# Placing tokens behind a step's first layer, with chunk 1's gates after the gathers and nine leading units

## What is computed

```
xn = layernorm(x)
s = group_norm(tanh(relu(rope(xn @ W_Q)) + hh_b))          # then turned
idx, w = route(xn)              # sigmoid, 4 of 8 groups, 6 of 32 experts, w sums to 2.5
gate[t, idx[t]] = w[t]
moe = sum_e gate[:, e] * (square(relu(xn @ W1[e].T)) @ W2[e].T)
shared = square(relu(xn @ Ws1.T)) @ Ws2.T
out = x + s * silu(shared + moe)
```

## Time and profile before

| | us |
|---|---|
| median of 3 runs | 337.94 |
| the runs | 333.05, 337.94, 338.01 |
| the profiled execution | 335.13 |
| its span in the trace | 333.3 |
| TensorE busy in it | 297.5 |

### The profile page before, as it was taken

One profiled execution on the slowest core, in us unless ns is written; L12 is line 12 of the kernel. 1 busy time (PEld: TensorE's weight loads), 2 busy tenths in 40 slices (PEclk: granted clock), 3 DMA queues, 4 the chain that ended last, 5 costly groups with the idle time before them and its releaser, 6 DMA issues.

```text
span 333.3 us, 6927 instructions
## 1 busy us (share of the span) xinstructions
PE 297.5 (89%) x2224; PEld 231.8 (70%) x2224; DVE 229.0 (69%) x585; ACT 179.3 (54%) x293; POOL 208.0 (62%) x226
## 2 busy tenths in 40 slices
PE   0577899879997999999999999998999999995994
PEld 0344666547776977888888698885767767785893
DVE  3788678887631378677778767687767576753774
ACT  3888598695452755557665576653363331212322
POOL 1874656681577777777777777304666777774640
PEclk9997899989997999999999999999999999995999
DMA  7455746722463376676766767555688777666552
GB/s 283 188 176 190 239 146 244 283 94 63 104 180 116 108 222 204 201 204 207 219 203 194 219 196 210 183 173 192 181 327 259 220 197 212 189 182 163 147 154 79
DMA packets 39651, 62.92 MB, mean 189 GB/s; under 512 B 5282, under 2 KB 25538, under 8 KB 39618
## 3 DMA queue, kind: packets, MB, share of 16 engines
q1 hardware_dynamic: 31794, 41.11, 37.2%
q0 software_dynamic: 7824, 21.38, 23.4%
HBM read 46.13 MB, written 16.33 MB: 187 GB/s over the span
## 4 chain that ended last, share of the span: by engine, by line
PE 56%; DMA 15%; POOL 8%; DVE 7%; ACT 6%; issue 6%; DVEq 1%; ACTq 0%
PE rot L962 12%; PE dp L990 10%; DMA yk<-ytab,slot 10%; PE rot L915 5%; PE hp L939 4%; DMA xgt<-xtab,ids 4%; POOL xgt L614 4%; PE hp L951 3%; PE hp L953 3%; PE hp L952 3%; POOL yk L623 3%; PE hp L941 3%; PE hp L940 3%; PE rot L975 2%; DVE xs L1265 2%
## 5 line engine op out<-in xcount | busy, mean ns | idle before, releaser
L614 POOL DMA_INDIRECT xgt<-xtab,ids x97 | 96.4, 994 | 39.7 <-issue 21.3
L680 ACT ACTIVATE hf<-hf 128x512 f32<-128x512 f32 (+2 forms) x74 | 45.8, 619 | 98.7 <-DVE hf L1246 74.8
L623 POOL DMA_INDIRECT yk<-ytab,slot x66 | 64.7, 980 | 44.3 <-DMA ytab<-late 17.1
L990 PE MATMUL dp<-w2s,hf 128*128 128x256 f32 x340 | 83.6, 391 | 4.3 <-issue 4.3
L990 PEld LDWEIGHTS dp<-w2s,hf 128*128 128x128 f32 x340 | 66.1, 198 | 16.2 <-issue 4.7
L694 ACT ACTIVATE xgt<-rot 128x1024 f16<-128x1024 f16 (+1 forms) x49 | 49.3, 1009 | 9.6 <-PE rot L915 9.2
L962 PE MATMUL rot<-w2s,hf 128*128 x194 | 51.3, 391 | 1.1 <-ACT xgt L694 1.0
L953 PE MATMUL hp<-xh,wlo 128*128 128x512 f16 (+2 forms) x148 | 45.0, 322 | 0.0
L952 PE MATMUL hp<-xh,whi 128*128 128x512 f16 (+2 forms) x148 | 45.0, 322 | 0.0
L951 PE MATMUL hp<-xh,whi 128*128 128x512 f16 (+2 forms) x148 | 44.9, 321 | 0.0
L1265 DVE SCALAR_TENSOR_TENSOR xs<-yk,wk,xs 128x256 f32<-128x256 f32 x66 | 32.0, 484 | 16.8 <-DMA yk<-ytab,slot 14.8
(11 more groups left out here) (162 smaller groups left out, 473.5 us busy)
## 6 DMA issues: line engine op xcount, KB each, us to landing
ytab<-late SPq DMA_DIRECT2D x48, 256.0 KB, 2.8
gate_bc<-gtab SPq DMA_DIRECT2D x40, 256.0 KB, 3.8
late<-in_w SPq DMA_DIRECT2D x17, 256.0 KB, 4.9
w2s<-in_w SPq DMA_DIRECT2D x8, 512.0 KB, 6.4
xs<-in_x SPq DMA_DIRECT2D x4, 512.0 KB, 4.7
xgt<-in_x SPq DMA_DIRECT2D x4, 512.0 KB, 6.5
out<-xgt SPq DMA_DIRECT2D x16, 128.0 KB, 3.7
xgt<-xtab,ids POOLq DMA_INDIRECT x97, 3.3
```

The lines of the kernel that those rows point to most:

```text
L614: nc.gpsimd.indirect_dma_start(xg[:, a % XRING, :], None, xtab, bass.IndirectOffsetOnAxis(ids[:, a:a + 1], 0))\
L623: nc.gpsimd.indirect_dma_start(yk[:, n % KRING, :], None, ytab, bass.IndirectOffsetOnAxis(slot[:, n // K, n % K:n % K + 1], 0))\
L990: mm = nc.tensor.matmul(dp[:, q // 2, q % 2, :], hf[:, k % HRING, cols], w2s[:, e, :], start=(e == 0 and q % 2 == 0), stop=(e == N - 1), s ...
```

## The change

PE's `place` moves from in front of `first(k)` to behind it, and one step earlier, so that the pair i = 0, 1 stands right behind `first(8)`, i = 2, 3 right behind `first(9)`, and so on. ACT's and DVE's side stays where it was. `weigh(1)` goes to step 19 on DVE, `gate_root(1)` behind POOL's 97 gathers, and the transpose, copy and store of these gates to steps 44 and 45. LEAD is 9: unit 17 of before (a dense unit) is done behind the slots, slot groups are units 17 to 41, and 32 dense units follow them in place of 31.

```diff
-LEAD = 10
+LEAD = 9
...
-        PLACE_AT = HOT_AT + 1
+        PLACE_AT = HOT_AT
...
-        GATES_AT = [4, PLACED - 1][0:len(BLOCKS)]
+        GATES_AT = [4, EARLY + LEAD + GROUPS + 2][0:len(BLOCKS)]
...
             if user_before[use]:
                 wait_left(engine, user_before[use])
             else:
                 engine.wait_ge(shared_out, len(shared_no))
                 engine.wait_ge(eoff_ready, 1)
-                engine.wait_ge(gt_ready, len(BLOCKS))
+                engine.wait_ge(gt_ready, 1)
...
             for s in range(1, POOL_STEPS):
                 low_w(s)
-                if s == POOL_STEPS - 3:
-                    for b in range(1, len(BLOCKS)):
-                        gate_root(b)
             pool.wait_ge(ids_ready, 1)
...
+            for b in range(1, len(BLOCKS)):
+                gate_root(b)
             for s in range(YRING):
                 pool.wait_ge(y_stored[s], 16 * len(range(s, len(slot_exits), YRING)))
...
+                elif f == 0:
+                    act.wait_ge(gt_stored, 16 * len(BLOCKS))
                 nc.scalar.activation(tz[:, f % 2, :], acc[:, j, :], ACT.Silu).then_inc(tz_ready, 1)
...
                 else:
-                    pe.wait_ge(shared_out, len(shared_no))
+                    wait_left(pe, last_user[0])
...
-                if 0 <= k - PLACE_AT < len(HOT_PAIRS):
-                    place(HOT_PAIRS[k - PLACE_AT])
                 if k + 1 < NU and UNITS[k + 1][0] == "slots" and len(leaves[k + 1]) > 1:
                     turn_slots(k + 1, 1)
                 if 2 <= k < NU and k != LAST + 1:
                     first(k)
...
                     bases()
+                if 0 <= k - PLACE_AT < len(HOT_PAIRS):
+                    place(HOT_PAIRS[k - PLACE_AT])
...
                 one_hot(i)
                 if i % 2 == 1 or i == NR - 1:
                     relu(HOT_AT + i // 2)
-                if i == 1:
-                    weigh(1)
```

More of the change, by code:

```diff
@@ L419, in build, with wait_left @@
             uses += [("leave", i, h) for i in leaving(k) for h in range(i != LAST, len(leaves[i]))]
-        use_no = {use: n for n, use in enumerate(uses)}
-        bank_of = {use: n % 3 for n, use in enumerate(uses)}
+        bank_of, user_before, last_user = {}, {}, {}
+        for n, use in enumerate(uses):
+            bank_of[use], user_before[use], last_user[n % 3] = n % 3, last_user.get(n % 3), use
+        def wait_left(engine, use):
+            what, k, h = use
+            if what == "turn":
+                engine.wait_ge(xt_copied, leaves[k][h][-1] + 1)
+            else:
+                wait_y(engine, store_no[k, h])
         def wait_bank(engine, *use):
-            n = use_no[use]
-            if n < 3:
+            if user_before[use]:
+                wait_left(engine, user_before[use])
+            else:
                 engine.wait_ge(shared_out, len(shared_no))
                 engine.wait_ge(eoff_ready, 1)
-                engine.wait_ge(gt_ready, len(BLOCKS))
[L430 to L435, removed]
+                engine.wait_ge(gt_ready, 1)
         @block.sync
@@ L798, in _ @@
                     high_w(s)
-                if k == PLACE_AT:
+                if k == PLACE_AT + 1:
                     act.wait_ge(branch_landed, 16 * 5)
@@ L1372, in _ @@
                 for s in range(POOL_STEPS, WSTEPS):
-                    if k == PLACED - 1 + (s - POOL_STEPS) // 2:
+                    if k == PLACED + (s - POOL_STEPS) // 2:
                         low_w(s)
-                for c in range(2, NCH):
+                for c in range(1, NCH):
                     if k == WEIGH_AT(c):
```

## The result

The changed kernel takes **344.06 us** (median of four runs: 342.86, 343.82, 344.30, 346.83), beside 337.69 us for the kernel before on the same chip (333.05 to 338.01). The ratio is **1.030, 95% interval 1.024 to 1.037**: slower. Run again on another chip (e5) it was 345.05 against 335.49 us, ratio 1.030 (1.023 to 1.036). I had forecast 341.5 us, inside 335 to 346.5, and put most of the chance on "within 2%". So the direction and the range held, and the size did not: 3.6 us above the kernel before's 337.94 was 1.1%, and 3.0% was measured.

What follows compares the result with a forecast made beforehand. TensorE, busy 297.5 of 333.3 us, was taken as the bound, with POOL pacing the gathers. Terms 2.5 + 0.8 + 2.9 = +6.2 us on 335.1 gave 341.3, stated as 341.5 us, range 335 to 346.5.

Steps and rivals of the forecast that it cites:

- within 2%: Class of results near the kernel before's time, with its slower border at about 342.3 us; chance 0.62.
- step 3: In the placing: two TensorE stops, each followed by half clock, cost +2.9 us, with ends 0 and 4.9.
- the scale: Whole span: the profiled execution's 335.1 us kept as base, though 2.8 us under the median shown; forecast 341.5 us.
- step 1: Nine leading units: nothing gained before the slots, the unit costs +2.5 us behind them, upper end 3.0.
- Step 2: Earlier place: ids, which starts the gathers, is ready at 86.7 us in place of 85.9, +0.8 us.
- my walk: Tracing of DVE's, ACT's and TensorE's queues through the placing: the last place ends at 85.5 us.
- third before the slots: Possible third half-clock stretch where TensorE waits for tile 7: +2 us in a rival of chance 0.22.
- the border of 342.3: Time in us at which the result would pass from within 2% to slower by more.
- Step 4: Chunk 1's gates behind the last gather: POOL ends them at about 222.3 us; cost 0 to 0.5, taken as 0.
- its cover: Spare time of 5 us on POOL between the late gates' end and the fetches, put at 227 us.
- The rule on the shared interfaces: By it, five one-hot pairs beside the gates would get lost time back; the sum gave this 0.
- the rival that an early list pays: Placing: if ACT's queue isn't the limit, ids comes at 82.4 to 84.1 us, total 334.1 to 335.8; chance 0.16.

Runs made afterwards that it cites:

- e5: The changed kernel run again, unaltered, on another chip: 345.05 us against 335.49 for the kernel before, ratio 1.030 (1.023 to 1.036).
- e1: The kernel before with only LEAD cut from 10 to 9: 338.26 us, ratio 1.009 (1.005 to 1.013).
- e7: The changed kernel with 21 spare matmuls ahead of the one-hot products of tiles 2, 3 and 4: 340.04 us, ratio 1.007 (1.002 to 1.013).
- e4: The changed kernel with ten leading units, so only place and chunk 1's gates moved against the kernel before: 342.36 us, ratio 1.017.
- e3: The kernel before with only chunk 1's gates moved late: 334.15 us where the kernel before took 336.26, no interval.
- e10: The kernel before with only chunk 1's gates moved late, on a chip with slower gathers: 370.58 us, ratio 0.996 (0.991 to 1.001).
- e12: The kernel of e10 with weigh(1) alone back in its old place on DVE: 373.96 us, ratio 1.001 (0.996 to 1.006).
- e13: The kernel before, unchanged, profiled again on a chip with slower gathers: first gather again 26.4 us behind the first product.
- e11: The changed kernel with ten leading units, place(2, 3) back behind the shared second layer, and ACT's one-hots 4 and 5 ahead of the splits: 370.73 us, ratio 0.994.
- e15: The changed kernel with place(2, 3) alone put back behind the shared unit's second layer, ACT's order kept: 378.45 us, ratio 1.008.

## Why the prediction was wrong, step by step

The mechanism was right: both stops, ACT behind PE's block and both stretches of half clock came. What failed is the size, in two places of the working: step 3's +2.9 for the half clock, and the scale, where a sum worked out from a low execution (335.1, 2.6 us under the median of 337.69) was given as a forecast of the median. The sum had 341.3; the profiled execution took 342.86. The 1.6 us between them are, rounded, 0.9 of head and 1.2 between first gather and first fetch, both taken as nothing, 0.7 more in the placing than steps 2 and 3 had, and 1.3 less at the end than step 1 had. The other 1.2 us to the median, 344.06, are scale.

- **Step 1, right in kind, 2.5 us.** Alone it is 3.0 by the ratio (e1), the upper end. In the changed kernel the last part is 1.2 and 1.8 us longer in its two traces: behind the first fetch TensorE is busy for 97.4 us in place of 94.9 and idle for 8.1 in place of 9.4. Its reason was partly wrong: TensorE didn't wait 3 us more before the slots (2.7 us idle against 2.0), since `place`, a step earlier, left a step more of work behind it.
- **Step 2, right in mechanism.** Stops of 0.68 and 1.56 us for the 0.9 and 1.8 that I had, 3.02 for 3.0; the second of ACT's copies ends at 72.1, where my walk had 69.4 at full clock, plus 0.9 of head and 1.8 of half clock. The first gather is 4.4 us later against the first product, where steps 2 and 3 had 3.7.
- **Step 3 failed in its size: half clock +2.9 us.** Both stretches came, in both traces of the changed kernel, and no third before the slots. But taking them away is worth 3.4 us up to the first gather, 3.8 between the profiled executions and 5.0 between the medians (e5 and e7). With 3.4 the sum is 6.7 and 341.8, still under the border of 342.3 that I had drawn; with 5.0 it is 8.3 and 343.4, over it. I had priced the half clock from one stretch of one execution, and took none of it to depend on the head. With a late head the old order is spared its own (24.8 in e1, whose code is the same up to there), and the changed one is not (30.4 in e4): 5.6 us apart there, 4.4 in the executions that were profiled first.
- **Step 4, cost nothing: its cover held.** TensorE's transpose didn't wait. But POOL ended the gates at 230.6, not 222.3, since 8.1 us pass between its first and second instruction there; without them the thirteen take 5.2 us, where beside the one-hots they took 10.1. That the gates' leaving gives nothing was true only of POOL's part: with `place` where it was, the move as a whole shortens placing by 3.7 us (e3, e10), of which my walk through DVE's queue had only `weigh(1)`'s 1.6 us on DVE and not the stop and the half clock that go with it. In the changed kernel this gain is buried under PE's order: 22.7 + 8.1 = 30.8.
- **The rule on the shared interfaces** (the Trainium skill, GPSIMD Engine Reference, Specifications: POOL contends with VectorE's instructions that read two SBUF inputs) would have brought the result nearer to the rival that an early list pays. e12 against e1 bounds what the thirteen instructions cost at 0.3 us. Beside the 128x512 split the hold was there again:

```profile
63.20 1.73 DVE L1289 TENSOR_TENSOR xgt<-iota,fa 128x588 f16<-128x588 f16 x1
```

- **The scale.** The profiled executions differ by 342.86 - 335.13 = 7.7 us: 0.9 in the head, 4.4 in placing, 1.2 up to the fetches, 1.2 at the end. But 342.86 is the lowest run of the changed kernel, and the profile of e5 is its lowest too, 1.2 and 1.4 us under their medians; the kernel before's, 335.13, stood 0.4, 1.1 and 2.6 us under its three medians on such chips (335.49, 336.26, 337.69). With the sum set on the median that I had been shown (337.94 + 6.2 = 344.1) the forecast would have met the measured 344.06, in part by luck, since its terms were off both ways. A forecast 0.8 us from the border of a class should not have had 0.62 on one side of it.

The 1.2 us between gathers and fetches stay unexplained. They lie behind the last gather (19.2 us to the first fetch in place of 18.0; the gathers themselves take 124.9 and 124.8), and the chips with slower gathers don't show them (170.4 for e13 and e10).

## What to carry to other kernels

Moving an instruction forward in an in-order queue moves everything behind it backward: ask of each operand when it will be there, and which block that someone else waits for is now queued behind the wait. In a queue of two waits that feed each other (PE for ACT's one-hots, ACT for PE's block), put what the other engine waits for first and work with slack last: the splits of two weights and W_Q's copy, moved behind two one-hots, gave 4 us. Stops of 2.2 and 3.0 us cost 3.4 to 5 us more in half clock, and the size of that has to be taken from several executions. And run the old order beside the mended one (e10 beside e11): it showed that the earlier `place` had nothing to give, even with its stops mended.

## What the runs showed of the hardware

- Spare matmuls (21 of 128x512) in place of standing still made the changed kernel 5 us faster between the medians.
- The same stop of 1.65 us is followed by a granted clock of 0.50 (the kernel before, e13) or 1.00 (e1, e12). In these four traces it is 1.00 where there was half clock between 48 and 56 us, and 0.50 where there was none. The longer stops of e4 and e15 are followed by half clock in spite of it.
- Between POOL's first two gate instructions stands a drain. Behind the 97 gathers 8.09 us pass there, in the changed kernel, e3 and e10 alike; in the kernel before, with no gathers ahead, the second of the two instructions starts at 64.47, 0.15 us behind the end of the first (63.54 + 0.78). It costs nothing here: POOL ends at 230.6, TensorE's transpose starts at 234.50 without a wait, and the fetches wait until 235.51.
- POOL's 128x32 instructions take 0.22 to 0.27 us each behind the gathers (one 0.58) and 0.25 to 0.96 us beside DVE's one-hots, while those one-hots lose 0.06 us at most. Beside a 128x512 split one of them takes 1.73 us in place of 0.76.
- One kernel takes 334 us on one chip and 371 on another, nearly all of it between the first gather and the first fetch (144 and 170 us) and behind (105 and 115).
